# Attention with the values as the stationary operand: three heads to a column group, and the sums transposed back

## What is computed

```python
# layer 0: queries are the normalised x, keys and values the context itself
energy = einsum('nqhd,nkhd->nhqk', q, k); energy = where(mask == 0, -1e20, energy)
out = einsum('nhqk,nkhd->nqhd', softmax(energy / sqrt(128)), v).reshape(N, Q, 128) @ W_out.T + b_out
# layer 2: two softmaxes over different projections, one set of values
diff = softmax(q1 @ k1 * s) - lambda_full * softmax(q2 @ k2 * s)
x = rms_norm(diff @ v1) * norm_w @ proj_w.T + proj_b
# layer 3: rotated q and k, a bias by position, and a gate
attended = (softmax(q @ k * s + bias) @ v) @ Wout.T + b_out
gate = sigmoid(attended @ Wgate.T + b_gate)
output = gate * attended + (1 - gate) * residual
```

## Time and profile before

| | |
|---|---|
| median of 3 runs | 1305.68 us (1291.06 to 1306.13) |
| profiled execution, its own time | 1308.73 us |
| its span | 1306.9 us |
| PE busy, PEld busy | 1077.4 us, 976.3 us |
| DVE, ACT, POOL busy | 670.0, 513.0, 397.4 us |
| mean granted TensorE clock | 0.814 of full |

### The profile page before, as it was taken

The page is one execution under the profiler, slowest core; times in us unless marked ns, Lnnn a source line. Parts: engine busy times, 40 slices in busy tenths (PEclk is TensorE's granted clock), DMA queues, the critical chain, the costliest instruction groups (busy, mean ns, idle before and its releaser), DMA issues. The chain is left out here.

```text
span 1306.9 us, 19893 instructions
## 1 busy us (share of the span) xinstructions
PE 1077.4 (82%) x7374; PEld 976.3 (75%) x7374; DVE 670.0 (51%) x1808; ACT 513.0 (39%) x987; POOL 397.4 (30%) x396
## 2 busy tenths in 40 slices
PE   3899999999988999889989762989169987359992
PEld 2888889999977899768888662888148877358882
DVE  7788511111257343667778643343567655444443
ACT  1443434444433334444444321655224323045552
POOL 4333300010013002300010054446634335545552
PEclk9866589999995899968788765999667656579996
DMA  9999800000000000000000013654200000155553
GB/s 324 170 172 170 156 1 1 1 1 1 1 1 1 1 1 1 1 1 1 1 1 2 1 33 115 177 172 147 65 1 1 1 1 20 36 168 174 174 165 97
DMA packets 70574, 83.52 MB, mean 64 GB/s; under 512 B 5297, under 2 KB 57528, under 8 KB 70352
## 3 DMA queue, kind: packets, MB, share of 16 engines
q1 hardware_dynamic: 64336, 71.71, 24.1%
q0 software_dynamic: 4992, 8.45, 1.9%
q10 hardware_dynamic: 1152, 2.10, 0.4%
HBM read 51.88 MB, written 32.18 MB: 64 GB/s over the span
## 5 line engine op out<-in xcount | busy, mean ns | idle before, releaser
L2167 ACT ACTIVATE hT<-PS,par 128x512 f32<-128x512 f32 x200 | 137.3, 689 | 186.4 <-PE PS L2115 184.9
L2207 DVE SCALAR_TENSOR_TENSOR X<-PS,wts,X 128x128 f32<-128x128 f32 x272 | 76.6, 344 | 231.5 <-PE PS L2127 231.5
L837 PEld LDWEIGHTS PS<-vblk,hT 128*128 128x128 f32 (+1 forms) x1152 | 175.1, 239 | 0.0
L1050 ACT ACTIVATE hT<-PS 128x512 f32<-128x512 f32 (+1 forms) x192 | 91.4, 490 | 205.0 <-PE PS L820 195.3
L837 PE MATMUL PS<-vblk,hT 128*128 128x27 f32 (+2 forms) x1152 | 170.3, 301 | 0.0
L820 PE MATMUL PS<-par,score 128*128 128x128 f32 (+1 forms) x640 | 135.8, 365 | 15.3 <-ACT score L1030 8.1
L820 PEld LDWEIGHTS PS<-par,score 128*128 128x128 f32 (+1 forms) x640 | 106.4, 190 | 25.2 <-issue 13.9
L2127 PEld LDWEIGHTS PS<-regA,hT 128*128 128x128 f32 x1024 | 119.2, 192 | 2.8
L2127 PE MATMUL PS<-regA,hT 128*128 128x128 f32 x1024 | 119.5, 275 | 0.0
L1097 POOL TENSOR_TENSOR score<-score,mx 128x1232 f32<-128x1232 f32 x32 | 72.0, 2249 | 121.7 <-DVE mx L922 121.7
L1878 PE MATMUL PS<-q_up,halves 128*112 128x256 f32 (+1 forms) x276 | 87.9, 318 | 16.1 <-DVE hT L1990 8.8
(11 more groups left out here) (301 smaller groups left out, 2108.9 us busy)
## 6 DMA issues: line engine op xcount, KB each, us to landing
regA<-L3f_w SPq DMA_DIRECT2D x23, 704.0 KB
regB<-L2f_w SPq DMA_DIRECT2D x23, 578.0 KB
L2f_sorted_x<-empty_row SPq DMA_DIRECT2D x8, 1161.0 KB, 21.9
L3f_sorted_x<-empty_row SPq DMA_DIRECT2D x8, 1161.0 KB, 22.1
regA<-L0f_w SPq DMA_DIRECT2D x4, 768.0 KB, 15.9
regA<-L2f_sorted_x SPq DMA_DIRECT2D x23, 129.0 KB, 3.7
regB<-L3f_sorted_x SPq DMA_DIRECT2D x23, 129.0 KB, 4.0
par<-params SPq DMA_DIRECT2D x1, 2386.0 KB, 12.2
```

What stands on the lines that cost most here:

```text
L837: last = nc.tensor.matmul(PS[:, 6, h0 * VW:(h0 + nh) * VW], pT, vblk[0:w, b, 3 * j * VW:(3 * j + nh) * VW], start=False, stop=j == NBLK - 1)
L1050: nc.scalar.activation(hT[:, u % 2, i, 0:full], PS[:, bank, 0:full], ACT.Copy)\
L2167: nc.scalar.activation(hT[:, n % 2, k, :], PS[:, i % 4, :], c["act"], bias=pc(f"{tag}_b1")[:, col:col + 1]).then_inc(h_ready.sem, 1)
```

## The change

- The values become the stationary operand and the transposed exps the moving one. Heads are put in six trios (the last has one head and two copies or empty places), 27 columns of values each, padded to 32. Trio g goes to column group g mod 4 of the array and so to PSUM partitions 32 (g mod 4) and on, in columns 0 to 127 for g below 4 and 128 to 255 above. Each trio's 231 keys are two overlapping blocks of 116, the last trio's 77 keys one: eleven blocks, `BLOCKS`, in an order that goes over the four groups. `vfull` is gone.
- The sums now come out transposed. ScalarE copies them to SBUF (`evacuate_sums`) and TensorE transposes them back in two products (`sums_back`), after the scores of the next unit but one. VectorE normalises from there.
- The copy of the transposed output (`evacuate_oT`) and, in L3x, that of the attended tile (`evacuate_attT`) move from VectorE to ScalarE. ScalarE's exps of the next unit move to behind the first of the three copies of transposes, and the routing's rows behind the second.
- VectorE normalises unit u - 1 between the two operations of unit u + 2's scores instead of unit u at the end; the addition to X becomes an operation of its own (`add_attended`), in L0x one unit later and also between the two.
- L3x has a lag of two as well, and its gate product takes turns in banks 4 and 5. The routing's and the normalisation's later parts (statistics, powers, scatters) move by a tile or two to fit.
- One product of the identity with itself fills half of bank 6 at each stage's start. The masks grow from 30 to 297 columns of the first parameter load.

```diff
-NBLK = -(-H * K // P)
...
+TRIO = 3
+NTRIO = -(-H // TRIO)
+BW = -(-TRIO * K // 2)
+FIRST_HALF = [TRIO * K * g for g in range(NTRIO)]
+SECOND_HALF = [TRIO * K * (g + 1) - BW for g in range(NTRIO - 1)]
+BLOCKS = [(g, FIRST_HALF[g], 0) for g in range(4)] + [(g, SECOND_HALF[g], 1) for g in range(4)]
+BLOCKS += [(4, FIRST_HALF[4], 0), (5, H * K - BW, 0), (4, SECOND_HALF[4], 1)]
...
-        vblk = sb("vblk", [P, B, NHM * VW])
-        vfull = sb("vfull", [P, B, H * VW])
+        vblk = sb("vblk", [P, B, NBLK, 32])
+        sums = sb("sums", [P, 2, P])
...
-            lag = 1 if tag == "L3x" else 2
+            lag = 2
...
-                    for j, (h0, nh, w) in enumerate(BLOCKS):
+                    for j, (g, _, half) in enumerate(BLOCKS):
                         if j % 4 == 0:
                             pe.wait_ge(pT_ready.sem, pT_ready.at(3 * u + j // 4 + 1))
-                        pT = hT[0:w, u % 2, j // 4, (j % 4) * P:(j % 4) * P + P]
-                        if j == 0:
-                            nc.tensor.matmul(PS[:, 6, 0:H * VW], pT, vfull[:, b, :], start=True, stop=False)
-                        else:
-                            last = nc.tensor.matmul(PS[:, 6, h0 * VW:(h0 + nh) * VW], pT,
-                                                    vblk[0:w, b, 3 * j * VW:(3 * j + nh) * VW],
-                                                    start=False, stop=j == NBLK - 1)
+                        slot, c = slice(32 * (g % 4), 32 * (g % 4) + 32), g // 4 * P
+                        last = nc.tensor.matmul(PS[slot, 6, c:c + P], vblk[0:BW, b, j, :],
+                                                hT[0:BW, u % 2, j // 4, (j % 4) * P:(j % 4) * P + P],
+                                                start=half == 0, stop=half == 1 or g == NTRIO - 1)
                     last.then_inc(o_psum.sem, 1)
+
+                def sums_back(u):
+
+                    pe.wait_ge(sums_ready.sem, sums_ready.at(u + 1))
+                    nc.tensor.transpose(PS[:, 6, 0:P], sums[:, 0, :], ident)
+                    nc.tensor.transpose(PS[:, 6, P:P + 64], sums[0:64, 1, :], ident[0:64, 0:64]).then_inc(o_back.sem, 1)
...
                     if u + 2 < units:
                         scores(u + 2)
+                    if 0 < u <= units:
+                        sums_back(u - 1)
                     done = after_unit(u)
...
-                for u in range(units + lag + (tag == "L3x")):
+                for u in range(units + lag + (sets == 1)):
                     done = after_unit(u) if u < units + lag else None
-                    if done is not None:
-                        if tag == "L2x":
-                            root_mean_square(done)
-                        evacuate_oT(done)
-                    if tag == "L3x" and u >= 2:
-                        gate_out(u - 2)
+                    if tag == "L2x" and done is not None:
+                        root_mean_square(done)
+                    before_last = u - lag - 1
+
+                    def between():
+                        if 0 < u <= units:
+                            normalise(u - 1)
+                        if sets == 1 and before_last >= 0:
+                            (gate_out if tag == "L3x" else add_attended)(before_last)
                     if u + 2 < units:
-                        maxima(u + 2)
+                        maxima(u + 2, between)
+                    else:
+                        between()
...
+                    if done is not None:
+                        evacuate_oT(done)
                     if u < units:
...
+                        evacuate_pT(u, 0)
                     if u + 1 < units:
                         exps(u + 1)
+                    if tag == "L3x" and done is not None:
+                        evacuate_attT(done)
+                    if u < units:
+                        evacuate_pT(u, 1)
+                        g = route["logits_group"](u) if route else None
+                        if g is not None:
+                            route["scalar_rows"](a, g, bank_of(("rows", g)))
+                        evacuate_pT(u, 2)
+                        evacuate_sums(u)
```

More of the change, by code:

```diff
@@ L739, in attention_stage @@
             o_psum = sem("o_psum", units)
+            sums_ready = sem("sums", units)
+            o_back = sem("o_back", units)
             o_used = sem("o_used", units)
@@ L774, in attention_stage @@
                     uses.append(("ranks", route["ranks_part"](u)))
+                if tag == "L3x" and u >= lag:
+                    uses.append(("gate", u - lag))
             turn_of = {use: i for i, use in enumerate(uses)}
@@ L785, in wait_for_bank @@
                 free = {"exps": pT_ready, "rows": route and route["rows_read"], "logits": route and route["logits_read"],
-                        "ranks": route and route["ranks_read"]}[kind]
+                        "ranks": route and route["ranks_read"], "gate": tag == "L3x" and g_in}[kind]
                 pe.wait_ge(free.sem, free.at(n + 1))
@@ new lines, in evacuate_pT, with evacuate_sums @@
+                def evacuate_pT(u, i):
+                    n, width = 3 * u + i, len(groups[i]) * P
+                    bank = bank_of(("exps", n))
+                    a.wait_ge(pT_psum.sem, pT_psum.at(n + 1))
+                    if i == 0 and u >= 2:
+                        a.wait_ge(o_psum.sem, o_psum.at(u - 1))
+                    nc.scalar.activation(hT[0:BW, u % 2, i, 0:width], PS[0:BW, bank, 0:width], ACT.Copy).then_inc(pT_ready.sem, 1)
+                def evacuate_sums(u):
+                    a.wait_ge(o_psum.sem, o_psum.at(u + 1))
+                    nc.scalar.activation(sums[:, :, :], PS[:, 6, 0:2 * P].rearrange("p (r q) -> p r q", r=2), ACT.Copy)\
+                        .then_inc(sums_ready.sem, 1)
@@ L1121, in pool @@
                         route["pool_tile"](p, st, t)
+                if tag == "L0x":
+                    after_nm["pool_group"](p, NG - 2)
                 if tag == "L3x":
-                    for t in range(NT - 3, NT):
+                    for t in range(NT - 4, NT):
                         less_xn(p, t)
@@ L1647, in pool_tile @@
                     pool_scatter(p, 0, range(at, at + 8))
-                if tag == "L3f" and t >= NT - 3:
-                    at = {NT - 3: 0, NT - 2: 2, NT - 1: 4}[t]
-                    pool_scatter(p, 0, range(at, at + 2))
+                if tag == "L3f" and t >= NT - 2:
+                    at = {NT - 2: 0, NT - 1: 3}[t]
+                    pool_scatter(p, 0, range(at, at + 3))
             def pool_tail(p, t):
+                if t == NT - 4:
+                    pool_power(p, late - 1)
+                    return
                 at = {NT - 3: 6, NT - 2: 9, NT - 1: 12}[t]
@@ L2408, in tables, with mask_of @@
     heads = np.arange(P)[:, None] // HD == np.arange(H)[None, :]
-    hmask = np.concatenate([(np.arange(P)[:, None] + j * P) // K == h0 + np.arange(min(3, NHM - 3 * j))[None, :]
-                            for j, (h0, _, _) in enumerate(BLOCKS)], axis=1)
+    def mask_of(j):
+        g, first, half = BLOCKS[j]
+        own = first + np.arange(BW)
+        own = np.where(own // (TRIO * K) == g, own, -1)
+        if half:
+            own = np.where(own >= FIRST_HALF[g] + BW, own, -1)
+        head = own[:, None] // K
+        return np.concatenate([head == (h if h < H else H - 1) for h in range(TRIO * g, TRIO * (g + 1)) for _ in range(VW)], axis=1)
+    hmask = np.zeros((P, NBLK * TW), bool)
+    hmask[0:BW] = np.concatenate([mask_of(j) for j in range(NBLK)], axis=1)
     wrap = np.arange(K + P)[None, :] % K == np.arange(K)[:, None]
```

197 lines of the change are left out of this document (86 added, 111 removed).

## The result

The changed kernel takes 1242.35 us (median of 4 runs, 1237.48 to 1243.91) and the kernel before, on the same chip, 1298.37 (4 runs, 1288.6 to 1306.13): a ratio of 0.957, interval 0.948 to 0.965. The profiled execution of the changed kernel took 1237.5 us, 71 less than that of before (1308.7). Some 15 of these 71 are the run and not the kernel, since the medians are 56 apart: over all its runs here the kernel before took from 1285.3 us at a mean granted clock of 0.834 to 1309.7 us at 0.816, and its profiled execution, at 0.814, is one of the long ones.

What follows compares the result with a forecast made beforehand. TensorE was taken to bound the attention units at either clock. L0x -13, L2x -13, L3x -29 and +6 for additions gave -49 from the profiled 1308.7 us: 1259.7, as a median 1257, range 1200 to 1335.

Steps and rivals of the forecast that it cites:

- A: The forecast itself: 1257 us, own range 1235 to 1278; chance 0.44.
- B: Rival: the clock rises with 128 columns moving, only a fifth of the units cold: -88, 1218 us; chance 0.20.
- +6 for what was added: Whole kernel: larger mask load, sums copy, turning back and handovers on each stage's last unit, more lag in L3x: +6 us.
- The bounds of 0.94 and 2.57 us: Weighted sum's 22 passes per unit at full clock: 0.94 us with complete overlap of column groups, 2.57 with none.
- the second pass waits for the first and holds back the next group: Weighted sum: each product costs one pass, so 12 passes, 1.40 us at full clock or 2.58 at half.
- The ring through ScalarE: Attention units at full clock: ScalarE's copies, exps and sums copy make a ring of 5.2 us, lengthening a warm unit.
- VectorE's chain of 5.1: L2x: the next scores wait for VectorE's score work and division, 5.1 us, level with ScalarE, hidden when cold.
- Keeping the present mix of clocks: Sum by stage: the warm share of units stays at 0.44 in L0x and L2x; L3x is colder.
- C: Rival: the clock falls because TensorE idles more whenever fast, all units cold: -2, 1304 us; chance 0.20.
- -15 for waits: L3x: TensorE's waits for VectorE before output transpose, projection and gate go, by the moved oT copy and longer lag: -15 us.
- the 6 us taken off for it: L0x: the X addition L978, placed before the maximum, misses GpSimd's shift, so TensorE's waits for it go: -6 us.
- D: Rival: no overlap, 32-column products in different column groups run one after another: +48, 1354 us; chance 0.16.

Runs made afterwards that it cites:

- e2: The changed kernel with the two products of a trio next to each other in the weighted sum's order: 1247.0 us, ratio 0.957 to the kernel before.
- e3: The changed kernel with ScalarE's exps of the next unit behind its three copies of transposes: 1228.1 us, ratio 0.943 to the kernel before.
- e5: The kernel before with 64 instead of 27 columns moving in the nine later blocks, the further ones zeros: 1282.1 us, ratio 0.990.
- e8: The changed kernel's schedule with the old weighted sum, 64 instead of 27 columns moving in its nine later blocks: 1260.5 us, ratio 0.972 to the kernel before.
- e10: e7 with eight further products that nothing reads, ahead of TensorE's wait for the routing rows: 1222.3 us, ratio 0.938 to the kernel before.
- e6: The changed kernel with the weighted sum of the kernel before, so the new schedule alone: 1288.1 us, ratio 0.994 to the kernel before.
- e7_again: The same kernel as e7, run again as the control of e10: 1229.1 us, ratio 0.943 to the kernel before.
- e4: The changed kernel with the copy of the transposed output back on VectorE: 1268.1 us, ratio 0.975 to the kernel before.
- e1: The changed kernel with the whole weighted sum of a unit computed twice: 1283.0 us, ratio 0.987 to the kernel before.
- e9: e1 with the order of e2, and the first of its two sums all in one column group: 1310.2 us, ratio 1.011 to the kernel before.
- e7: e3 with the norm's subtraction and square sum in L2x moved behind VectorE's score subtraction: 1223.5 us, ratio 0.945 to the kernel before.

## Why the prediction came out as it did

I forecast 1257, 3.7% less; it was 1242, 4.3% less. The time is inside the range and inside A's own; the reasons are partly B's. Against the profiled execution the sum was -49 and it was -71, by the medians -56. By stage the sum had -13, -13 and -29 for L0x, L2x and L3x and +6 for what was added; the units give -17, -29 and -26, and no run measured the +6.

- **The weighted sum.** The bounds of 0.94 and 2.57 us were right: 0.90 was measured, and 2.45 for 22 passes in one group. The step that chose between them failed: "the second pass waits for the first and holds back the next group", twelve passes, 1.40. e2 shows that nothing is held back, and the 22 passes take what the fullest group needs, eight. That is 0.5 us too much, and it decided nothing, because the next step was right:
- **The ring through ScalarE.** Forecast 5.2 us, measured 5.08; TensorE waits for the hT copy, as said, and e3 takes the ring away (4.49). In L2x VectorE's chain of 5.1 stood behind it, at 5.07 in every second unit. So the warm unit got longer, 4.57 to 5.08, and a shorter weighted sum could not show there.
- **The clock.** "Keeping the present mix of clocks" is the step that was wrong at the root. The share of warm units was to stay at 0.44; the stages went from 0.70, 0.76, 0.65 to 0.90, 0.94, 0.83. Warm units got longer and the mean unit shorter, since few are cold now: in L2x 5.56 us against the forecast 6.1, 17 us over 32 units. B had this, for the reason that e5 and e8 bear out: more columns moving than 27, and the clock higher with nothing else changed in the stages. The objection that I raised against B, and the case C built on it, was that a warm TensorE would idle 1.3 us of 5.2; it waits some 0.65 at a time and stays warm, while behind the 1.96 us of a routing unit the clock does fall, and not when they are filled (e10). By time the moving columns were the larger effect (e6 to e8 28 us, e7_again to e10 7).
- **B's sizes.** B had L0x 5.6, L2x 5.5 and -38 in L3x, and -88 in all. L0x and L2x came to 5.52 and 5.56, its numbers. L3x gave 26 and not 38.
- **L3x.** The forecast had -14 for the units and -15 for waits, 29 in all, and 26 came, but with the clock's rise in it (0.65 to 0.83). So without that the units and waits gave less than the 29. The wait that I named in the trace, the projection behind VectorE's copy, is shown by e4; the other two were only argued. L3x keeps other waits, 8.5 us for the hT copy and 4.7 for the scores, and its warm unit is 5.76 us (one start of the scores to the next), not 5.2.
- **L978.** Its successor L982 takes 306 ns on the mean in L0x, forecast 0.29: right. But the 6 us taken off for it are not shown to have come. TensorE waited 6.3 us in five waits for L978 before and waits 6.9 us in five waits for the division (L951) now; the order that frees the one puts the other late.
- **C and D.** D fell with the timelines of e1 and e9: in four groups the passes do overlap. C's fall of the clock did not come. By the rule of the Trainium skill ("TensorE: Matmul & The Clock Gate", Part 4: PE-mode transpose) three more passes of transposes spoke for it; the clock rose, and no run isolates the transposes.
- **Signs.** Under 1.1 us for the passes was given as the sign of complete overlap, and a clock well above as that of B: both came. The other signs, 5.2, the hT copy, L978 and no wait before L3x's projection, came as A had them. The 7.1 of a unit at half clock was not read.

So the number was near because the ring, sized right, bounds the warm unit whichever overlap one takes, and in part by luck. The forecast left out the clock, which gave more, and took off L978's 6 us and up to 15 of waits in L3x that came only in part or not at all; the two errors run against each other. The 7 us that the sum lacks by the medians, and 22 by the profiles, are what is left of them. Not tried: the new weighted sum in the old schedule, which would measure the layout without the moved copies.

## What to carry to other kernels

Price a new layout at both granted clocks and then ask what it does to the clock itself. Here passes bound by their weight load, with 27 columns moving, kept TensorE 95% busy at a granted clock of 0.69, and the same number of passes with 64 (zeros even) had 0.91 (e6, e8). When products are spread over column groups, count the passes of the fullest group. When products become shorter, look for the ring through the copying engines, since it sets the next bound; here ScalarE's exps stood in it and could be moved behind the copies for 1%. Then read the next ring over two units: e7 made every second one shorter and the others longer. A wait of two microseconds on TensorE cost 2 and 3 us more behind it at two places of L2x, and eight useless products in it saved that; over the whole program they gave 7 us.

## What was not expected of the hardware

- TensorE 95% busy at a granted clock of 0.69 (e6), and 86% busy at 0.91 with 64 instead of 27 columns moving (e8).
- Two column groups run beside each other even when each one's two products are adjacent in program order (eight passes in 0.48 us, e2), and with four groups 22 passes of 128 columns take 0.88 us, 0.040 each, weight load included, against 0.111 in one group (e1, e9).
- A wait of 1.95 us, and another of 0.45 behind it, were followed by some 10 us at half clock (e7, about 595 to 606 us); with the first filled with products, by none (e10).
